# Moving one kernel's projection to stationary weights, with queries and keys stacked by DMA over device memory

## What is computed

```
xn = layernorm(x)                                  # 2048 x 256
q = rope(xn @ Wq)   # 8 heads of 32;   k = rope(xn @ Wk), v = xn @ Wv   # 2 heads of 32, each used by 4 q heads
std = softmax(causal(q @ k.T / sqrt(32))) @ v
geo = softmax(causal(qp[:, None] * kp[None, :])) @ v      # qp = q[..., :3] . dir_h,  kp = k[..., :3] . dir_h
attn = (std + head_scale * (geo - std)) @ Wo
z = xn @ ternary(W_syn).T + b_syn                  # 2048 x 1024
hidden = where(z >= (102nd largest of the row), relu(z), 0)
ffn = layernorm(xn + hidden @ ternary(W_out).T + b_out) * gamma + beta
out = x + attn + ffn
```

## Time and profile before

| | |
|---|---|
| median of 3 runs | 773.45 us (772.93 to 773.46) |
| profiled execution, its own time | 772.55 us |
| its span | 770.6 us |
| busy: PE / DVE / ACT / POOL | 699.5 / 499.1 / 464.7 / 262.5 us |
| mean granted TensorE clock | 0.936 of 2.4 GHz |
| DMA traffic | 9.40 MB |

### The profile page before, as it was taken

One profiled execution on the slowest core, in us unless ns is written; L12 is line 12 of the kernel. 1 busy time (PEld: TensorE's weight loads), 2 busy tenths in 40 slices (PEclk: granted clock), 3 DMA queues, 4 the chain that ended last, 5 costly groups with the idle time before them and its releaser, 6 DMA issues. The chain is left out here.

```text
span 770.6 us, 12758 instructions
## 1 busy us (share of the span) xinstructions
PE 699.5 (91%) x4536; PEld 327.3 (42%) x4536; DVE 499.1 (65%) x1022; ACT 464.7 (60%) x789; POOL 262.5 (34%) x390
## 2 busy tenths in 40 slices
PE   2766789999999999999999999999899999988993
PEld 1443335333434444443444445444445455553532
DVE  3798478764386886377777873655776666667602
ACT  3352655335753544875443547888889889868650
POOL 5514453332431312331101203324424533356532
PEclk9885889698999999999999999899999999999996
DMA  8100000000000000000000000000000000000000
GB/s 240 61 1 4 6 1 8 1 1 3 1 8 1 1 1 1 3 1 1 6 3 1 1 1 10 1 1 8 16 7 9 8 8 15 8 8 2 1 1 27
DMA packets 12372, 9.40 MB, mean 12 GB/s; under 512 B 5713, under 2 KB 11729, under 8 KB 12306
## 3 DMA queue, kind: packets, MB, share of 16 engines
q1 hardware_dynamic: 12306, 8.55, 3.8%
HBM read 5.80 MB, written 2.10 MB: 10 GB/s over the span
## 5 line engine op out<-in xcount | busy, mean ns | idle before, releaser
L731 ACT ACTIVATE probs<-scores 128x1024 f32<-128x1024 f32 (+3 forms) x320 | 270.0, 893 | 202.9 <-PE acc L1216 188.3
L929 DVE TENSOR_REDUCE piece_max<-side 128x1 f32<-128x512 f32 x192 | 127.9, 686 | 54.5 <-PE side L1110 53.3
L1209 PE MATMUL acc<-probs,v_nat 128*32 128x512 f32 (+3 forms) x1280 | 157.1, 564 | 5.3 <-POOL probs L608 3.9
L1216 PE MATMUL acc<-probs,ones_all 128*32 128x512 f32 (+3 forms) x1280 | 155.4, 558 | 0.0
L608 POOL TENSOR_SCALAR_AFFINE_SELECT probs<-probs 128x256 f32<-128x256 f32 x128 | 56.3, 451 | 184.1 <-ACT probs L731 182.7
L1110 PE MATMUL side<-k_stack,q_stack 96*128 96x512 f32 (+3 forms) x290 | 112.6, 442 | 3.9 <-DVE piece_max L929 3.6
L1191 PE MATMUL scores<-q_stack,k_stack 98*128 98x512 f32 (+3 forms) x320 | 90.2, 384 | 5.6 <-ACT probs L731 5.3
L1110 PEld LDWEIGHTS side<-k_stack,q_stack 96*128 96x128 f32 x290 | 51.4, 194 | 96.2 <-DVE piece_max L929 45.2
L955 DVE RECIPROCAL d_raw<-d_raw 128x512 f32<-128x512 f32 x16 | 53.6, 3347 | 34.7 <-ACT o_raw L744 34.7
L1191 PEld LDWEIGHTS scores<-q_stack,k_stack 98*128 98x128 f32 x320 | 53.0, 190 | 36.0 <-ACT probs L731 27.1
L1195 PE MATMUL scores<-q_geo,k_geo 10*128 10x512 f32 (+3 forms) x320 | 58.0, 468 | 6.6 <-ACT probs L731 6.3
(11 more groups left out here) (143 smaller groups left out, 1024.5 us busy)
## 6 DMA issues: line engine op xcount, KB each, us to landing
res<-in_L_attn_x_dram SPq DMA_DIRECT2D x4, 512.0 KB, 9.2
out_dram<-res SPq DMA_DIRECT2D x16, 128.0 KB, 1.7
z_buf<-in_L_ffn_W_syn_dram SPq DMA_DIRECT2D x1, 1024.0 KB, 7.7
z_buf<-in_L_ffn_W_out_dram SPq DMA_DIRECT2D x1, 1024.0 KB, 4.8
k_geo<-geo_rows SPq DMA_DIRECT2D x24, 8.0 KB
q_geo<-geo_rows SPq DMA_DIRECT2D x24, 8.0 KB
w_qkv<-in_L_attn_Wq_dram SPq DMA_DIRECT2D x1, 256.0 KB, 4.2
tables<-in_cos_table_dram SPq DMA_DIRECT2D x1, 256.0 KB, 4.5
```

Of the source, the lines that this page charges most:

```text
L731: nc.scalar.activation(probs[:, slot % 2, pair, :, off:], scores[:, pair, :, off:], ACT.Exp, scale=ATT_SCALE if kind == 0 else 1.0).then_i ...
L929: free(nc.vector.tensor_reduce(piece_max[:, h, p:p + 1], pt, AX.X, ALU.max), ("S",) + a)
L1209: nc.tensor.matmul(acc[D * h:D * h + D, 0, off:], v_nat[:, j, g], probs[:, slot_no[a] % 2, h // 2, h % 2, off:], start=(j == 0), stop=(j = ...
L1216: last = nc.tensor.matmul(acc[D * h:D * h + D, 1, off:], ones[:, 0:D], probs[:, slot_no[a] % 2, h // 2, h % 2, off:], start=(j == 0), stop ...
```

## The change

The projection turns round. Four tiles of `xn` are transposed together (`xT`, 2 units of 4 transposes per chunk), and the weights become stationary: 128 of their columns (`qA`, `qB`, `qK`), with 512 tokens streaming, so q and k come out transposed, with the dimension on partitions. For this the weights are first sorted on VectorE (`w_sort`), first halves of all heads together, then second halves, so that the rotary step is an elementwise product of whole tiles with a transposed table of angles. That table (`trig`) is built on the chip: 12 units `tT` of four transposes of spread angles, parked in device memory for chunks 1 to 3. v keeps the old form (`v`: 4 tiles, 64 columns). The geometric dot products become a matmul with a small matrix of directions (`gx`). The high and low parts are written to device memory (`khi_park`, `hi_park`, `klo_park`, `lo_park`) and read back into the 96 stacked rows (`stack_hi`: 4 DMAs, `stack_lo`: 2). The transposes L1093, L1099 and L1101 are gone. `xn` and `xnT` are kept for one chunk only and parked too; each ternary tile reads its parts back (`xz_in`, `xb_in`), which replaces the second transpose. The maximum of the geometric scores is now formed on VectorE alone, and the constants of `k_geo`/`q_geo` are set on VectorE instead of GpSimd.

In the plan the ternary tiles get a turn each, spread over the slots of attention (LEAD, REACH), `pick` and `hide` get rank 2 instead of 5 and 4, and TURN becomes a table of 145 to 235 ns, counted before a start is compared with others.

```diff
-TURN = 110
+TURN = {("full", "columns"): 235, ("rows", "columns"): 215, ("columns", "full"): 145, ("columns", "rows"): 145,
+        ("full", "rows"): 220, ("rows", "full"): 220}
+LANDING = {"m_dma": 2300, ..., "khi_park": 2200, "klo_park": 2200, "hi_park": 3500, "lo_park": 3500, "stack_hi": 6000,
+           "stack_lo": 4500, "xz_in": 2300, "xb_in": 2300}
...
-            unit("qkv", 2 * c, ("xT", t), 220, [("xn", t)])
-            unit("qkv", 2 * c, ("qkv", t), 1300, [("xnT", t)] + [("w",)] * (t == 0) + [("unit", "kT", t - 2)] * (t > 1))
-            add("rope", "dve", 0, ("rope", t), 1380, [("unit", "qkv", t)] + [("join", t - 1)] * (t > 0),
-            add("rope", "dve", 0, ("split", t), 1050, [("join", t), ("q_twin", t)] + old[1:])
-            add("twin", "act", 1, ("q_twin", t), 620, [("join", t)] + old[:1])
-            for half in range(2):
-                unit("heads", 2 * c, ("qT", t, half), 440, [("split", t), ("q_twin", t)])
-            unit("heads", 2 * c, ("kT", t), 440, [("split", t), ("geo_dots", t)])
+        for s in "ABK":
+            unit("proj", 2 * c, ("q" + s, c), 1790, [("xnT", c, 0), ("xnT", c, 1)] + [("w_sort",)] * (c == 0))
+            add("rope", "dve", 0 if c == 0 else ROPE_RANK, ("rope", c, s), 1250, [("unit", "q" + s, c)] + ...
+        unit("proj", 2 * c, ("v", c), 1250, [("xnT", c, 0), ("xnT", c, 1)])
+        unit("gx", 0, ("gx", c), 1780, [("join", c, "A"), ("join", c, "K")] + [("dirs",)] * (c == 0))
+        add("split", "act", 1, ("hi", c), 1130, [("join", c, "A"), ("join", c, "B")])
+        add("split", "dve", 0 if c == 0 else ROPE_RANK, ("lo", c), 1170, [("hi", c), ("unit", "gx", c)])
+        add("stack", "sp", 0, ("stack_hi", c), 2200, [("khi_park", c), ("hi_park", c)]
+            + ([("sum", c - 2, G - 1, 0, TPC * (c - 1) - 1)] if c >= 2 else []))
+        add("stack", "sp", 0, ("stack_lo", c), 1100, [("klo_park", c), ("lo_park", c)])
...
+    for t in range(NT):
+        due = LEAD + REACH * t / NT
+        turn.append(next(slot for n, slot in enumerate(slots) if sum(share[:n + 1]) >= due * sum(share)))
...
-            start = max(ready, clock[eng])
+            start = max(ready, clock[eng] + (TURN.get((mode, m), 0) if eng == "pe" else 0))
...
+                    for r in ((1,), (0, 2))[1 - part]:
+                        sp.dma_start(k_stack[D * r:D * r + D, :, cols].bitcast(F32),
+                                     k_parked[c, part].rearrange("(d g) t -> d g t", g=G)).then_inc(stack_in[c], 16)
+                    for r in ((2,), (0, 1))[1 - part]:
+                        sp.dma_start(q_stack[D * r:D * r + D, b].bitcast(F32),
+                                     q_parked[c, part].rearrange("(d h) t -> d h t", h=H)).then_inc(stack_in[c], 16)
...
+                        for i in range(KC):
+                            last = nc.tensor.matmul(pt, w_qkv[:, i, at:at + P], xnT[:, i], start=(i == 0), stop=(i == KC - 1))
```

More of the change, by code:

```diff
@@ new lines, in build_plan @@
+        add("geo_in", "act", 0, ("geo_in", c), 1200, [("unit", "gx", c)]
+            + [("geo_hi", c - 1), ("geo_top", c - 1), ("geo_lo", c - 1)] * (c > 0), empties=("gx", c))
+        add("split", "act", 1, ("khi", c), 600, [("join", c, "K")])
+        add("split", "act", 1, ("hi", c), 1130, [("join", c, "A"), ("join", c, "B")])
+        add("split", "dve", 0 if c == 0 else ROPE_RANK, ("klo", c), 620, [("khi", c), ("unit", "gx", c)])
+        add("split", "dve", 0 if c == 0 else ROPE_RANK, ("lo", c), 1170, [("hi", c), ("unit", "gx", c)])
@@ L180, in build_plan, with held_up @@
             emptied_by.setdefault(o[4], []).append(key)
[L181 to L186 removed]
+    ahead = {}
+    for keys in queue.values():
+        ahead.update(zip(keys[1:], keys))
+    def held_up(key, own):
+        if key in done or key not in op or key == own:
+            return False
+        if op[key][0] == "pe":
+            return True
+        return any(held_up(d, own) for d in op[key][2] + ((ahead[key],) if key in ahead else ()))
     bank = {}
@@ L225, in build_plan @@
                     after = after + (other,)
-            if any(d not in done for d in gates.get(key, ())):
+            if key[0] == "unit" and any(held_up(r, key) for r in emptied_by[key[1:]]):
                 continue
@@ L896, in _ @@
                 if k == "scan":
                     c, kp = a[0], geo_row[:, 0]
[L898 to L899 removed]
+                    consumed(dve, ("gx", c))
                     settle()
```

638 lines of the change are left out of this document (407 added, 231 removed).

## The result

| | before | after |
|---|---|---|
| median of 4 runs | 773.19 us (770.77 to 773.46) | 778.84 us (778.08 to 783.38) |
| ratio, 95% interval | | 1.0094, 1.0068 to 1.012 |
| profiled execution, span | 772.55, 770.6 us | 778.08, 776.3 us |
| mean granted clock | 0.936 | 0.929 |
| first geo score of chunks 0, 1, 2, 3 | 86.4, 138.3, 277.0, 474.1 | 65.2, 146.4, 279.0, 494.3 |

A ratio counts only the fast runs of a kernel, here those within 1.5% of its fastest one.

A forecast was written before the change was run, and what follows sets the result against it. TensorE (PE), busy 91% of the span, was taken as the bound. Span 770.6 - 6 (work) - 12 (shape changes) - 8 (start) = 744.6, plus 1.95 around it: 746 us; 730 to 756 at 0.50, 728 to 774 for 8 in 10.

The forecast's parts named there:

- The start: Up to chunk 1's geo attention: less idle PE gains 4 us, less half-clock work 4, together 8.
- near 30: Sign at the start: PE's idle time before chunk 1's geo attention, 38.6 us before, falls to near 30.
- PE's work: Transposes and projection on PE: 49.3 us before, 43.3 after with v and gx, a gain of 6 us.
- The rule weighed beside the start: Throttled clock is the default: the start until 48 us runs at 1.2 GHz throughout, making the sum 5 us worse.
- Changes of shape: PE's list, mostly chunk 2's and 3's attention: 129 fewer changes at 0.13 to 0.16 us; 12 us taken.
- My end of 0: Lower bound for the shape-change gain: every change saved turns into waiting, gaining 0 us; the upper end was 21.
- Rival 2: Stacks stand behind q_geo rows in SP's queue; PE waits up to 15 us a chunk, 791 us; chance 0.18.
- the mark: Sign of rival 2: waits of S for a DMA onto the stacks after 100 us, above 5 us in all.
- the mild case: Rival 2 with two thirds of its 45 us of waiting: 776 us.
- The chance of "slower": Whole kernel slower than before by more than two runs' agreement of 1.5 us: chance 0.14.
- The other marks: Wrong if chunk 3's geo attention begins after 474 us or its stage shortens under 4; PE busy about 680.

The follow-up runs named there:

- e3: Changed kernel with the loads of angles and Wq, Wk, Wv issued by SP right behind the first x, not by ScalarE; 768.04 us, ratio 0.9956.
- e4: Changed kernel with the planner's stack landing times at 10000 and 9000 ns, not 6000 and 4500; 766.12 us, ratio 0.9915.
- e5: Changed kernel with both the early loads on SP (e3) and the longer stack landing times (e4); 754.41 us, ratio 0.9765.
- e2: Kernel before with only the new rule: the price of a shape change takes part in choosing PE's next instruction; 781.83 us, ratio 1.0114.
- e1: Changed kernel with the old rule: shape-change price of 110 added after PE's instruction is chosen; 781.46 us, ratio 1.0122.
- e13: e3 with all instruction lists otherwise fixed, two of three 512 KB copies into q_stack left out for chunks 2 and 3; 764.10 us, ratio 0.9862.
- e14: Kernel before with HAND, the planner's cost of a hand-over, at 165 and not 160; 777.52 us, ratio 1.0034.
- e15: Changed kernel with HAND, the planner's cost of a hand-over, at 165 and not 160; median 791.41 us, ratio 1.0137.
- e16: e5 with HAND, the planner's cost of a hand-over, at 165 and not 160; 771.93 us, ratio 0.9965.

## Why the prediction was wrong

The sum gave a span of 744.6 us and it was 776.3, 31.7 more. By the account 9.6 of this lie in the start, 22.7 in what was taken back from the changes of shape, and the rest is within 0.5.

1. **The start, forecast -8, was +1.6** (64.2 to 65.8 us above the work up to chunk 1's geo attention), and here the cause is shown. The prediction priced ScalarE's compute and set "xn could be ready at 14 as before ... about 18". It left out the five issues on ScalarE's own queue, 13.5 us of them, and the landing of the tables: the first spreading began at 19.06, the first `xn` at 22.58 and the projection at 29.69, where 19.1 was forecast. From there the estimated chain holds: projection to first geo score took 35.5 us, 35.9 were forecast (19.1 to 55). e3 prices the step at 10.8 us, e4 against e5 at 11.7, and with it mended the start gains 6.9, near the forecast. The geo attention of chunk 1 began 8.1 us later and not near 130, and PE's idle time before it was 37.8 us (38.6 before), where "near 30" was to be seen.

2. **PE's work, forecast -6, was right:** transposes and projection are 50.5 us before (29.5 + 21.0) and transposes, projection, `v` and `gx` 44.0 after (8.5 + 20.6 + 7.1 + 7.8), by prices at full clock: 6.5 less, where 49.3 and 43.3 stood. The rule weighed beside the start, that it would run at 1.2 GHz throughout (the Trainium skill, "TensorE: Matmul & The Clock Gate", section "What's actually happening"), is mostly what the trace shows: of the 45.4 us from the first matmul to the first geo score 31.7 were at half clock, 11.8 of them ahead of the clock's first record. Before had 44.9 of 74.1.

3. **Changes of shape, forecast -12, is the step that failed by most.** By the account it was +10.7: 10.3 us less work, and 21.0 more above it behind the start. The work side was nearly right: 10.3 us by the account (16.8 less the 6.5 of item 2), 0.08 to 0.10 a change in the pairs and not 0.13 to 0.16. What failed is "12 us of it count". The waits in the last stage were taken as the only place where a PE that comes sooner waits longer, and chunk 2's attention was put at nothing. There the time above the work rose from 4.2 to 26.7 us. The new rule alone brings it to 20.7 (e2), the rest of the change alone to 16.7 (e1), and in five of five pairs grouping brought more excess at full clock. My end of 0 was no end: the kernel before loses 1%. Why the excess comes back, beyond the 5.0 us of item 4, stays open.

4. **Rival 2, stacks late,** had the right wait and the wrong reason. S waited for stacks 3.3 us at 64.6, 0.3 at 132.1 and 5.0 at 339.0; the mark was 5 us behind 100 us, and 5.3 just passes it. e13 gives 4 to 7 us for most of it, where the mild case had 30. At chunk 3 full DMA engines held the stack up and not SP's queue: 512 KB of `q_stack` took 7.3 us from issue to landing at the median, where the earlier trace rows has 4.8 for 1 MB. (The chances give rival 2 a third, 0.06, below the time of before, but only 0.01 + 0.03 of it enter the sum.)

5. **What no case had** is the scatter between orders of the same work, 0.3% to 2%. Chunk 2's attention took 18.2 us more: 4.3 less work, and 22.5 more above it, of which 5.0 are the wait for the late stack and 9.1 excess at low clock. In e2 grouping makes that stage 7.0 longer (204.1 for 197.1), but e1, with the old rule, has 218.7, so the new projection lengthens it without the grouping. As an estimate from e14, e15 and e16, a forecast of a change that reorders everything needs 3 us to each side for this alone, and up to 15. The chance of "slower", 0.14, was too small by it.

6. **The other marks.** Chunk 3's geo attention began at 494.3; later than 474 was to mean "wrong", and it does. The stage from there on became shorter (by 14.8, 4 was the mark), but 12.8 of it is work that stands elsewhere or is gone, and 1.6 is excess. PE's busy time fell to 695.6 and not 680. The spreading did nothing for the last stage: the first `hide` stands at 476.0 (464.6 before), with chunk 3's last maximum. PE's waits and the time give no sign that work taken off ScalarE and GpSimd bought anything.

```profile
476.04 1.28 DVE L1250 SCALAR_TENSOR_TENSOR work<-z_buf,thresh 128x1024 f32<-128x1024 f32 x1 [1.27 <-DVEq L1247]
```

The best order found comes near the forecast of 746: e5, whose only edits to the change are the place of five loads and two numbers of the planner, ran at 754.4. Of the 24.4 us between it and after, 10.8 to 11.7 are shown to be the loads. What the landing times gave is not assigned: the late stack was worth 4 to 7 in e3's order, but e5 with HAND at 165 has no late stack to mend and is at 771.9. So 754.4 is one good order, and the ten kernels with early loads stand at 0.992 in the mean, some 767 us.

## What to carry to other kernels

Price the issues of a queue and the landing of its loads as the first step of every chain that they feed; small rows that were issued on a second queue beside big loads landed 17.7 us later here, and 6.2 later when they went ahead of them in one. Before a stage between two events is called longer or shorter, count the work that was done in it: the plan may have moved some across the cut. Check the clock that a view reports by the step of two like matmuls. Where a scheduler writes the order, disturb it by a number that means nothing and time that first: differences below that scatter say nothing about an edit, and an edit is then tested with all lists fixed, as e3 and e13 were. Keep the planner's landing times at what the trace shows under load.

## What the runs showed of the hardware

A load with rows of 128 bytes on ScalarE's queue landed after 17.7 us beside 3 MB of large loads on SP's, and after 6.2 when it stood ahead of them in one queue; behind it the issue of a load of 256 KB held ScalarE for 8.23 us, on SP the same issue took 1.18. TensorE began at half clock in every kernel here, after 8.8 to 19.9 us without a matmul, and kept it for 3.7 to 22.6 us (steps of 0.213 us a transpose, 0.109 at full clock). It ran at half clock while busy for 13.70 of 13.70 us (e2), so a full busy share doesn't keep the clock up. Of one kernel the runs scattered by 1.4% (e4: 760.96 to 771.58), of another by 0.3% (e5).
